# Graph-attention kernel: a rebuilt score path and schedule, with the ELU sum and the low part of the normalised rows on VectorE

## The reference, cut to what matters

```python
h  = x @ W_fc.T ;  f1 = h @ a1 ;  f2 = h @ a2
s  = leaky_relu(f1[:, :, None] + f2[:, None, :], 0.2)
s  = where(adj == 0, -1e9, s)
x1 = layernorm(x + elu(softmax(s) @ x))
xn = x1 / sqrt(max(sum(x1 * x1), 1e-12))
x2 = layernorm(x1 + (xn @ xn.T) @ adj @ x1)
```

## Time and profile before

| quantity | value |
|---|---|
| median of 3 runs | 388.94 us (388.8 to 389.22) |
| span of the profiled execution, first to last instruction | 387.4 us |
| median of the runs less that span | 1.54 us |
| busy: PE, DVE, ACT, POOL | 87%, 92%, 76%, 64% |

### The profile page before, as it was taken

The page is one execution under the profiler, slowest core; times in us unless marked ns, Lnnn a source line. Parts: engine busy times, 40 slices in busy tenths (PEclk is TensorE's granted clock), DMA queues, the critical chain, the costliest instruction groups (busy, mean ns, idle before and its releaser), DMA issues. The chain is left out here.

```text
span 387.4 us, 7628 instructions
## 1 busy us (share of the span) xinstructions
PE 335.1 (87%) x2244; PEld 306.2 (79%) x2244; DVE 357.0 (92%) x951; ACT 293.9 (76%) x623; POOL 246.9 (64%) x320
## 2 busy tenths in 40 slices
PE   2387699998989899898989899898989899899892
PEld 1276698988889798888889798878879798889781
DVE  3999799999999999999999999999999999989524
ACT  2578395978969697887969697887969697886551
POOL 5301747776768787676867687676877687665311
PEclk9997889999999999999999999999999999999997
DMA  7531005051240707042150706033160705001013
GB/s 220 165 106 56 1 18 147 3 166 52 70 150 3 217 2 216 1 133 84 44 172 0 217 0 190 27 113 103 19 200 0 218 1 165 0 2 55 2 54 108
DMA packets 25527, 33.87 MB, mean 87 GB/s; under 512 B 896, under 2 KB 17312, under 8 KB 25504
## 3 DMA queue, kind: packets, MB, share of 16 engines
q0 software_dynamic: 8448, 16.78, 15.3%
q1 hardware_dynamic: 17056, 16.81, 13.8%
HBM read 25.20 MB, written 8.39 MB: 87 GB/s over the span
## 5 line engine op out<-in xcount | busy, mean ns | idle before, releaser
L816 PE MATMUL ps_h<-x_hi,probT_hi 128*128 128x256 f32 x256 | 79.9, 312 | 18.6 <-DVE probT_lo L410 15.0
L817 PE MATMUL ps_h<-x_lo,probT_hi 128*128 128x256 f32 x256 | 74.0, 289 | 0.0
L818 PE MATMUL ps_h<-x_hi,probT_lo 128*128 128x256 f32 x256 | 73.7, 288 | 0.0
L394 DVE CUSTOM_DVE_ANT_0 score_sb<-score_sb,neg_base 128x512 f32<-128x512 f32 x64 | 72.8, 1153 | 0.7 <-ACT score_sb L618 0.6
L816 PEld LDWEIGHTS ps_h<-x_hi,probT_hi 128*128 128x128 f32 x256 | 50.1, 196 | 22.8 <-DVE probT_lo L410 17.7
L881 PE MATMUL ps_l<-w_sb,xnT 128*128 128x256 f32 x256 | 61.6, 385 | 6.9 <-DVE y L463 6.7
L852 PE MATMUL ps_l<-xn_hi,adj_sb 128*128 128x256 f32 x256 | 62.9, 286 | 0.9 <-DVE xn_lo L433 0.9
L853 PE MATMUL ps_l<-xn_lo,adj_sb 128*128 128x256 f32 x256 | 62.4, 284 | 0.0
L881 PEld LDWEIGHTS ps_l<-w_sb,xnT 128*128 128x128 f32 x256 | 46.1, 190 | 18.0 <-DVE y L463 11.7
L870 PE MATMUL ps_l<-xn,z_sb 128*128 128x256 f32 x256 | 60.2, 379 | 0.0
L382 DVE SCALAR_TENSOR_TENSOR neg_base<-adj_sb,f_row 128x512 f32<-128x512 f32 x64 | 58.3, 914 | 0.0
(11 more groups left out here) (64 smaller groups left out, 724.1 us busy)
## 6 DMA issues: line engine op xcount, KB each, us to landing
adj_sb<-adj POOLq DMA_DIRECT2D x16, 1024.0 KB, 5.9
x_sb<-x SPq DMA_DIRECT2D x16, 512.0 KB, 4.5
out<-o_sb SPq DMA_DIRECT2D x15, 512.0 KB, 3.3
out<-o_sb SPq DMA_DIRECT2D x2, 256.0 KB, 2.3
attn_cols<-w_attn SPq DMA_DIRECT2D x2, 0.1 KB, 1.6
wfc<-w_fc SPq DMA_DIRECT2D x1, 32.0 KB, 1.8
```

The source lines that it names most:

```text
L394: nc.vector.tensor_tensor_reduce(out=score_sb[:, c, :], in0=score_sb[:, c, :], in1=neg_base[:, c, :], scale=1.0, scalar=LOWEST, op0=ALU.su ...
L816: nc.tensor.matmul(ps, probT_hi[:, c, blk], x_hi[n][:, k, :], start=(k == 0), stop=False)
L817: nc.tensor.matmul(ps, probT_hi[:, c, blk], x_lo[n][:, k, :], start=False, stop=False)
L818: last = nc.tensor.matmul(ps, probT_lo[:, c, blk], x_hi[n][:, k, :], start=False, stop=(k == NC - 1))
```

## The change

The program is written anew with one loop over `STEPS = range(-3, B + 3)`, fully unrolled; each helper returns at once where its graph does not exist, so that the first and last graphs have no code of their own. What it does otherwise:

- Scores: `make_mask` turns `adj` into 0 or -2^100 in bf16, one instruction of 2048 elements; `masked_f2` adds it to f2 straight from PSUM and takes the row maximum, four of 512; `lrelu` on ScalarE adds f1 and applies leaky ReLU in place (`Prelu`). `base`, `score`, `copy_f2` and `relu_z` go.
- `negate_max` moves from GpSimd to VectorE, two small dependent instructions for each half graph.
- `x_hi` is no longer copied by ScalarE but loaded from memory a second time, by a converting DMA in GpSimd's queue.
- The ELU sum (`residual_sum`) and `xn_lo` (`split_xn`) move from GpSimd to VectorE. GpSimd keeps `split_x`, one `pow` of 8 columns (`power`) in place of two of 4, the products `norm`, and `power2`, `shift2`.
- The sums around the powers (`moments`, `ve2`, `neg_mean2`) move to VectorE; `normalise` takes mean and 1/norm directly.
- The order of every queue changes. The last graph's halves, split between two engines before, are gone.

```diff
+            def make_mask(g):
...
+                dve.wait_ge(adj_in[n], 16 * (r + 1))
+                nc.vector.tensor_scalar(mask[:], adj_sb[n][:].bitcast(F32), -1.0, MASKED, ALU.add,
+                                        ALU.mult).then_inc(mask_ok, 1)
...
+                nc.vector.tensor_tensor_reduce(
+                    out=score[:, c, :], in0=mask[:, c, :], in1=ps_f2[:], scale=1.0, scalar=LOWEST,
+                    op0=ALU.add, op1=ALU.max, accum_out=row_max[:, c:c + 1]).then_inc(score_ok, 1)
...
+                dve.wait_ge(score_ok, NC * g + 2 * half + 2)
+                nc.vector.scalar_tensor_tensor(out=neg_z[:, c], in0=row_max[:, c], scalar=-1.0, in1=f[n][:, 0, c],
+                                               op0=ALU.mult, op1=ALU.subtract).then_inc(neg_z_ok, 1)
+                dve.wait_ge(neg_z_ok, 2 * g + half + 1)
+                nc.vector.scalar_tensor_tensor(out=neg_max[n][:, c], in0=neg_z[:, c], scalar=SLOPE, in1=neg_z[:, c],
+                                               op0=ALU.mult, op1=ALU.min).then_inc(neg_max_ok, 1)
...
-                pool.tensor_tensor(y[n][:], y[n][:], exp_h[:], ALU.add).then_inc(y_ok, 1)
+                nc.vector.tensor_tensor(y[n][:], y[n][:], exp_h[:], ALU.add).then_inc(y_ok, 1)
...
-                pool.tensor_tensor(xn_lo[n][:], xn[n][:], xn_hi[n][:].bitcast(F32),
-                                   ALU.subtract).then_inc(xn_lo_ok, 1)
+                nc.vector.tensor_tensor(xn_lo[n][:], xn[n][:], xn_hi[n][:].bitcast(F32),
+                                        ALU.subtract).then_inc(xn_lo_ok, 1)
...
+            def load_x_hi(g):
...
+                if graph(g - NBUF):
+                    pool.wait_ge(h_ps, NC * (g - NBUF + 1))
+                    pool.wait_ge(x_lo_ok, g - NBUF + 1)
+                pool.dma_start(x_hi[g % NBUF][:], x_rows[g]).then_inc(x_hi_in[g % NBUF], 16)
...
+            for i in STEPS:
+                load_x_hi(i + 2)
+                norm(i)
+                load_adj(i + 3)
+                split_x(i + 2)
+                power2(i - 1)
+                shift2(i - 1)
+                power(i + 1)
...
+            for i in STEPS:
+                residual2(i - 2, 1)
+                masked_f2(i + 1, 2)
+                negate_max(i + 1, 0)
+                residual2(i - 2, 2)
+                split_xn(i - 1)
+                residual2(i - 2, 3)
+                masked_f2(i + 1, 3)
+                node_scores(i + 2, 1)
+                residual(i)
+                residual_sum(i)
+                negate_max(i + 1, 1)
+                row_moments2(i - 2)
+                probT_lo_part(i + 1, 0)
+                row_moments(i)
+                node_scores(i + 2, 0)
+                probT_lo_part(i + 1, 1)
+                denominators(i + 1)
+                normalise(i)
+                probT_lo_part(i + 1, 2)
+                make_mask(i + 2)
+                probT_lo_part(i + 1, 3)
+                masked_f2(i + 2, 0)
+                residual2(i - 1, 0)
+                masked_f2(i + 2, 1)
```

More of the change, by code:

```diff
@@ L72, in program @@
[L72 to L84, removed]
+        x_sb = ring("x_sb", [P, NC, D], F32)
+        x_hi = ring("x_hi", [P, NC, D], F32R)
+        x_lo = ring("x_lo", [P, NC, D], F32R)
+        adj_sb = ring("adj_sb", [P, NC, N], F32R)
+        xn = ring("xn", [P, NC, D], F32)
+        xn_hi = ring("xn_hi", [P, NC, D], F32R)
+        xn_lo = ring("xn_lo", [P, NC, D], F32R)
@@ new lines, in split_x, with power @@
+            def split_x(g):
+                if not graph(g):
+                    return
+                n, r = g % NBUF, g // NBUF
+                pool.wait_ge(x_in[n], 16 * (r + 1))
+                pool.wait_ge(x_hi_in[n], 16 * (r + 1))
+                pool.tensor_tensor(x_lo[n][:], x_sb[n][:], x_hi[n][:].bitcast(F32), ALU.subtract).then_inc(x_lo_ok, 1)
+            def power(g):
+                if not graph(g):
+                    return
+                n = g % NBUF
+                pool.wait_ge(moments_ok, 2 * (g + 1))
+                pool.tensor_tensor(powers[n][:], moments[n][:], minus_half[:], ALU.pow).then_inc(powers_ok, 1)
@@ L452, in normalise, with residual_sum @@
-            def normalise(i, n):
-                dve.wait_ge(norm_ok, i + 1)
-                for c in range(NC):
-                    last = nc.vector.tensor_scalar(xn[n][:, c, :], y[n][:, c, :], xn_scale[:, c:c + 1],
-                                                   xn_bias[:, c:c + 1], ALU.mult, ALU.add)
-                last.then_inc(xn_ok, 1)
-            def residual2(b, n, c):
-                dve.wait_ge(o_ps, NC * b + c + 1)
+            def residual_sum(g):
+                if not graph(g):
+                    return
+                n = g % NBUF
+                dve.wait_ge(q_ok, g + 1)
+                nc.vector.tensor_tensor(y[n][:], y[n][:], exp_h[:], ALU.add).then_inc(y_ok, 1)
@@ L927, in _ @@
-            run_steps(pe, step)
+            for i in STEPS:
+                attend(i, 2)
+                attend(i, 3)
+                make_out(i - 2, 3)
+                for c in range(NC):
+                    make_z(i - 1, c)
+                transpose_prob(i + 1, 0)
+                for d in range(DC):
+                    transpose_xn(i - 1, d)
+                make_w(i - 1, 0)
+                make_w(i - 1, 1)
+                transpose_prob(i + 1, 1)
+                transpose_prob(i + 1, 2)
+                make_out(i - 1, 0)
+                attend(i + 1, 0)
+                make_out(i - 1, 1)
+                transpose_prob(i + 1, 3)
+                bcast_f2(i + 2)
+                attend(i + 1, 1)
+                make_out(i - 1, 2)
```

864 lines of the change are left out of this document (326 added, 538 removed).

## The result

| | median of the runs | range | span of the profiled execution |
|---|---|---|---|
| before, beside it (4 runs) | 389.07 us | 388.8 to 389.22 | 387.4 us |
| changed kernel (4 runs) | 397.83 us | 396.55 to 398.84 | 395.5 us |

The ratio is 1.0219, with a 95% interval of 1.0194 to 1.0244. The change makes the kernel slower, by some 8.8 us. The forecast of 370, and the range that ended at 392, were wrong.

The account below looks back on a forecast made before the run. VectorE was taken as full, with 4.4 us of its 21.97 a graph spent waiting for GpSimd. Head 55.1 + 13 x 20.7 + tail 44.4 = 368.6 of span, plus 1.5, gave 370 us; range 362 to 392.

Parts of the forecast that it names:

- the wait for `probT_hi`: VectorE, ahead of `probT_lo`: waits 0.45 us in every graph for ScalarE's `probT_hi`.
- Head and tail: Time up to graph 1's statistics, 55.1 us, and from graph 14's statistics to the end, 44.4 us.
- VectorE's own work: VectorE's instructions per graph without waiting for GpSimd: 19.9 us after the change, against 17.6 before.
- Four `normalise`: VectorE's four normalisations per graph, priced at 1.3 us, unchanged by the change.
- The mask: VectorE's new instruction of 2048 elements, priced at 1.13 us, two elements a cycle.
- rival 1: Mask on VectorE runs at one element a cycle: period 20.7 + 1.07, time 385 us; chance 0.14.
- The way from `xn_lo` to `probT_lo`: From VectorE's `xn_lo` end through TensorE and ScalarE until `probT_lo` can start: about 7.5 us.
- Rival 3: Memory traffic from reading `x` twice: a wait of 1 to 1.5 us a graph, 387 us; chance 0.07.
- the margin: Between the end of VectorE's ELU sum and negation (t + 5.0) and GpSimd's `x_lo` start (5.4): 0.4 us.
- rival 2: GpSimd's `x_lo` lands on VectorE's ELU: period 22.9 to 23.4, time 401 us, slower; chance 0.24.
- The price of the collision: Wait when VectorE's ELU sum or negation meets GpSimd's `x_lo`: 2.39 us less its own overlap, every graph.
- TensorE's floor: TensorE's matmuls, transposes and hand-offs: 20.1 us a graph, which no order gets below; 362 us in time.

Follow-up runs that it names:

- Experiment 1: Changed kernel with VectorE's second negation of the row maximum put ahead of the two ELU instructions; 371.45 us.
- e2: Changed kernel with only 4 of the 1024 columns of `x_lo` made from graph 3 on; 367.81 us.
- e7: Experiment 1 with the two small sums of the second layer's statistics (`ve`, `neg_mean`) behind the first `probT_lo`; 370.01 us.
- e10: Experiment 1 with the ELU sum alone moved back to GpSimd, behind the products of the norms; 372.84 us.
- e9: Changed kernel with `x_lo` made in two instructions, 16 columns first and the other 1008 behind them; 398.16 us.
- e3: Changed kernel with `x_lo` ahead of the load of `adj` in GpSimd's queue, with the same wait for `make_z`; 386.77 us.
- e8: Experiment 1 with `xn_lo` back on GpSimd behind the norm products, and `ve` and `neg_mean` behind the first `probT_lo`; 353.86 us.
- e4: Changed kernel with the ELU sum and `xn_lo` both back on GpSimd, ahead of the load of `adj`; 375.47 us.
- e5b: Changed kernel with a `pow` of 3 columns put between the load of `adj` and `x_lo` on GpSimd; 384.77 us.

## Why the prediction was wrong

**The sum was near, in part by luck.** Experiment 1, the change with one pair of instructions elsewhere, has 371.45 against a forecast of 370, and its period is 20.74 against 20.7. But in its middle the wait for `probT_hi` that the sum had at 0.45 doesn't occur, and the hold of `ve`, which the sum didn't have, stands in its place with 0.75. The kernels without either hold, e2 and e7, have 20.50 and 20.65 in the middle, so the sum was within 0.2 of what it stood for. The terms one by one:

- Head and tail: graph 1's statistics at 55.34 (55.1 in the sum), the tail 395.5 less 350.99, or 44.5 (44.4). The tail's terms as listed add up to 44.8 and not to 44.4, a slip of 0.4 in the adding.
- VectorE's own work: 22.91 less the 2.86 of holding is 20.05 with its small hand-offs, where the sum had 19.9 and 0.35.
- Four `normalise`: 1.3 in the sum, 1.6 in the middle (218.03, 1.67 less the overlap). GpSimd makes the two products of `norm` meanwhile (218.67 and 218.96, 0.2 each); no run takes them apart, so the cause is not shown.
- The mask, 1.21 in the trace for 2048 elements, as the 1024 of `y` take 1.22: two elements in the time of one, so rival 1 was false.
- The wait for `probT_hi`: 0.45 in the sum, 0.38 in e2. The way from `xn_lo` to `probT_lo`: 7.5 in the sum, 7.44 in e10.
- Rival 3: `node_scores` doesn't wait for `x` in the steady middle, so memory traffic cost nothing there.
- The median less the span of its profile, 1.5 in the sum, was 2.3.

**The step that failed** is the margin in rival 2: "VectorE's ELU sum and the negation behind it ... end at t + 5.0. The margin is 0.4." Both times were nearly right. With t as the end of `xn_lo` (203.52), `x_lo` starts at t + 5.33 (5.4 in the text), and the first negation would have ended at t + 4.86 and the second at about t + 5.05. What was wrong is the assumption that any margin ahead of that start is free. Behind a DMA issue the hold reaches at least 0.47 ahead of it (changed kernel, e9), which is more than the margin of 0.4 that I gave. So the collision needed no delay at all, where I made it depend on one, with a chance of 0.24. Once in it, the kernel stays in it, since both instructions follow from the same t, as the rival said: 22.91 was measured for its 22.9 to 23.4, and 397.83 for its 401.

A margin of 0.4 in a cycle of 20.7 for a loss of 2.4 to 2.9 is a coin, not a forecast of one in two against one in four. That should have been weighed without knowing of the early hold.

**The price of the collision** was set at 2.39 less an overlap; it is 2.86 in the changed kernel. In e3, with no DMA issue ahead, it is 2.16.

**One forecast was too cautious.** TensorE's floor was put at 20.1; the kernels that reach it show 19.41. I had added 0.4 of hand-offs, and in e8 TensorE has no gap for them; and I had priced `attend` at 0.122 a matmul, where in e8 one starts 0.117 behind the other (22 steps from 197.31 to 199.87), which makes 0.26 on 48. That is all but a few hundredths of the 0.7. "No order gets below it" was wrong for that reason, and 362 as the lowest time as well: 353.86 was reached.

**Small instructions.** I had counted `ve`, one of which stands in each period, as free of the port. It was held for 0.75 in experiment 1, 1.2 in e4 and 1.6 in e5b.

## What to carry to other kernels

When work is moved off GpSimd to spare VectorE the shared port, look at where the large instructions that remain will stand against VectorE's smallest ones: a 128x2 negation that meets a 1024-element instruction costs as much as a large one, and it meets it again in every period if both follow from the same event. Treat a margin of half a microsecond as none, above all behind a DMA issue in GpSimd's queue, and put the small two-input instructions ahead of the long VectorE work rather than behind it. Then ask for each move which loop the instruction lies in: `xn_lo` on VectorE closed a loop through TensorE and ScalarE and cost 16 us (371.45 to 355.21), so this part of the change was a loss by itself. The ELU sum lay in the slack of the same loop, and while `xn_lo` stayed on VectorE it cost the same on either engine (371.45 and 372.84, with intervals of the ratio that overlap).

## What the runs showed that I had not expected

- The hold of the port begins ahead of the traced start of a large GpSimd instruction that follows a DMA issue: 0.45 and 0.47 ahead were held, 0.60 and 0.65 ahead were free, and behind a `pow` 0.45 ahead was free.
- The wait goes both ways. In e4 GpSimd's `xn_lo` lasts 2.83 in the middle and 2.40 in the last graphs (332.64), where VectorE makes no mask; in the row below VectorE's mask had begun 0.65 ahead of it and ended at 208.68. That the mask is the cause fits these times and `x_lo` in e3, and was not tested apart. The row of GpSimd:

```profile
208.12 2.83 POOL L263 TENSOR_TENSOR xn_lo<-xn,xn_hi 128x1024 fp32r<-128x1024 f32 x1 [1.71 <-ACT xn_hi L500]
```

- A sum on one fp32 tensor with one constant, 128x4, waits for the port like an instruction with two inputs (`ve`: 0.91, 1.36 and 1.74 in place of 0.17, each ending within 0.04 of the end of `x_lo`). The prediction had the two rules at hand that say so: the Trainium skill (VectorE: DVE Perf Modes, Mode 2×_2P) lets a one-source fp32 `tensor_scalar` between SBUF tensors use both read ports, and the Trainium skill (SBUF — State Buffer, Who interferes with whom) has such an instruction wait for a GpSimd one that issued first. I applied them to the mask and to `normalise`, and not to an instruction of four columns; these rows agree with them.
